# A two-layer gated Flamingo block on one Trainium2 core: the second attention's keys and values are made between the products of the first FFN, and its slot is written as one list per engine

## The chip, the cores and the metric

The kernel runs on one core of one Trainium2 chip, as one launch. The metric is device time in microseconds, the median over several executions. Matrix products in full precision are made here from two rounded parts of each operand (hi and lo) in three passes of TensorE.

## The reference, cut to what matters

```python
# x (16, 256, 256), ctx (16, 77, 256)
x = x + tanh(g_xattn[0]) * L0_xattn(layernorm(x), ctx)   # 16 heads of 16
x = x + tanh(g_ffn[0])   * L0_ffn(layernorm(x))          # quantised, hidden 768
x = x + tanh(g_xattn[1]) * L1_xattn(layernorm(x), ctx)   # 8 heads of 64
x = x + tanh(g_ffn[1])   * L1_ffn(layernorm(x))          # butterfly, hidden 1024

def L0_ffn(x):        # act_qdq: round(v / s) * s with s = max|v| / 32767 over the whole tensor
    x = act_qdq(x); up = act_qdq(x @ qdq(w_up).T); gate = act_qdq(x @ qdq(w_gate).T)
    gate = act_qdq(gate * u16(sigmoid(gate)))
    return act_qdq(gate * up) @ qdq(w_down).T
def L1_xattn(x, ctx): # no biases but bo
    q, k, v = x @ Wq, ctx @ Wk, ctx @ Wv                 # inner width 512
    return softmax(q k^T / 8) v @ Wo + bo
```

The keys and values of the second attention depend on ctx and the weights alone, so nothing of x has to be ready for them.

## The kernel before, in words

`build` calls four stages in order: the first attention (`stacked_attention`), the quantised FFN (`quantised_ffn`), the second attention (`attention` with layer=1) and the butterfly FFN (`butterfly_ffn`). x stays in SBUF as xres: 16 batches (b) of 256 rows, two tiles of 128. Each stage is a chain of blocks; in a block every engine has its own in-order program, and engines meet at semaphores. A block ends when all its engines have ended. A product of two fp32 operands is `three_passes` (L39 to L41): hi by hi, hi by lo, lo by hi.

**Down phase**, the last block of the quantised FFN (L2005 to L2178). f_hid holds the product of gate and up. Per batch DVE makes the codes (L2052, f_ocode), ACT rounds them to f_o_hi (L2093), DVE subtracts to f_o_lo (L2057), TensorE makes the down product of the batch, 2 tiles x 6 chunks x 3 passes = 36 matmuls, and DVE adds it to xres (L2064). Between these, ACT and POOL combine the outer butterfly matrices (f_y, f_z) for the last FFN (L2123, L2128, POOL's sums L2028); TensorE's nine small products for them stand around the first two batches. SP stores f_z and f_y to w_spill (L2034, L2036). hid is laid out by chunk: [128, 6, 4096].

**Setup** of the second attention (one block). SP loads the weights a_w_raw (L954), ctx a_c_raw (L958), a_wo_raw (L962) and small operands (bias, gate, mask, pick). ACT rounds, DVE splits (L1027 is ctx's lo part). TensorE makes 12 key products, 4 chunks of the inner width by 3 column groups of ctx (412, 410, 410 columns), each 6 matmuls; ACT and DVE keep them as a_k_hi (L1006) and a_k_lo (L1036). Then 16 value products, one per batch, 77 rows x 512, 6 matmuls each, copied by DVE to a_values (L1049), which POOL has cleared (L980). Meanwhile DVE and POOL make the layer norm of batch 0 (statistics L892, L897; inverse root L903, L905; normalised a_xn L910). ACT loads the table for Exp at L1009.

**Slot loop** (one block, `slots`). The 16 batches are run through a software pipeline. One slot is one list of steps, the same for every engine; an engine does those steps of it that are its own:

```python
            SLOT = ("s0 s1 xt kb p0 q0 at0 q1 s2 p1 mx0 at1 s3 mx1 p2 mx2 p3 mx3 ln pr0 norm mt xn pr1").split()
            slot(-1, 1, middle=False, back=False)
            slot(0, 0, back=False)
            with eng.Fori(0, (B - 4) // 2) as j:
                slot(j * 2 + 1, 1)
                slot(j * 2 + 2, 0)
            slot(B - 3, 1)
            slot(B - 2, 0, pre=False)
            slot(B - 1, 1, pre=False, front=False)
            slot(B, 0, pre=False, front=False, middle=False)
```

In slot b the scores and sums of batch b are made; ln and xn belong to batch b+2, the front steps (xt, kb, q, mx, mt) to batch b+1, the back steps (at, pr) to batch b-1. The steps are: ln, statistics of x on DVE (L892, L897) and their inverse root on POOL (L903, L905); xn, the normalised rows on DVE (L910), after which POOL adds the gated bias to xres (L918); xt, four transposes of xn (TensorE L1356, ACT hi L1219, DVE lo L1287); q0 and q1, the queries in two halves of 12 x 2 matmuls (a_w_hi; ACT L1226, DVE L1296, two operations each); kb, the masked keys of the batch (DVE's hi half, POOL's lo half, both L1160); mx0 to mx3, a cheap single-pass score product (L1380) whose maxima over the 77 keys DVE takes (L1304); mt, their transposes (L1388), copied by ACT (L1231) to a_mt; s0 to s3, the scores of two heads each, in which a fourth matmul takes the maxima off (a_pick by a_mt), and their Exp on ACT (L1238, a_prob); p0 to p3, the sums over keys by values (L1417); norm, the division on DVE (L1260 to L1273); at0 and at1, transposes of the result (L1431, ACT L1243, DVE L1310); pr0 and pr1, the projection, 24 matmuls a half (a_wo_hi), whose result DVE adds to xres (L1318) in pr1. s0 waits for a_mt.

## Time and profile before

| what | value |
|---|---|
| median of 3 executions | 1223.14 us (1222.58 to 1225.68) |
| profiled execution, its own time | 1222.77 us |
| its span | 1221.0 us, mean granted TensorE clock 0.926 |
| busy: PE, DVE, ACT, POOL | 85%, 67%, 48%, 21% |
| down phase | 582 to 663 us |
| setup of the second attention | 667 to 717 us |
| its slots | 717 to 998 us |

Times in the rows are microseconds from the start of the span. Where an engine was idle before an instruction, the row ends with that idle time and what released it. The granted clock is a share of TensorE's full speed, 1.00 being 2.4 GHz.

### The profile page before, as it was taken

What the parts mean: (1) busy time and instruction counts of PE and PEld (TensorE: products, weight loads), DVE (VectorE), ACT (ScalarE), POOL (GpSimd) and SP (SyncE); (2) the same over time, 40 slices, a digit from 0 to 9 for tenths busy, and PEclk for the clock granted to TensorE, in tenths of its full rate; (3) what the DMA queues carried; (4) which work ended last, traced back from release to release, by engine and by line L of the source; (5) the groups of instructions that cost most, each with busy time, mean ns of one, the idle gap of its engine ahead of it and who ended that gap; (6) DMA issues with size and microseconds to landing.
All of it is one profiled execution on the core that took longest, in us unless ns stands there. A gap on an engine that the chain in (4) does not pass through costs nothing. (4 is left out here: it accounts for less than half of the span.)

```text
span 1221.0 us, 20807 instructions
## 1 busy us (share of the span) xinstructions
PE 1033.3 (85%) x7125; PEld 903.3 (74%) x7125; DVE 820.3 (67%) x1700; ACT 580.8 (48%) x1028; POOL 261.4 (21%) x454
## 2 busy tenths in 40 slices
PE   6499999998389988366996779999999967999998
PEld 5367777776378866256996658999999956888888
DVE  5357787864458898798685745666666638676562
ACT  3256666665377699697463403333333314232220
POOL 4313333311176000000023112222221203211110
PEclk9689999998689999677998889999999988999999
DMA  6735555561233177697001200000000020000001
GB/s 191 210 93 130 129 129 129 130 191 36 78 140 138 44 250 250 238 308 254 35 0 70 90 1 1 1 0 0 0 0 0 1 77 2 18 18 18 20 32 35
DMA packets 50765, 106.50 MB, mean 87 GB/s; under 512 B 6688, under 2 KB 25120, under 8 KB 48400
## 3 DMA queue, kind: packets, MB, share of 16 engines
q1 hardware_dynamic: 50400, 104.61, 27.3%
q0 software_dynamic: 304, 1.10, 0.3%
q8 instruction: 35, 0.57, 0.2%
q14 instruction: 26, 0.21, 0.1%
HBM read 63.64 MB, written 39.52 MB: 84 GB/s over the span
## 5 line engine op out<-in xcount | busy, mean ns | idle before, releaser
L39 PE MATMUL bank<-f_xt_hi,f_w_hi 128*128 128x512 f32 x320 | 130.6, 408 | 16.2 <-DMA f_xt_lo<-x_spill 9.5
L41 PE MATMUL bank<-f_xt_hi,f_w_lo 128*128 128x512 f32 x320 | 127.7, 399 | 0.0
L40 PE MATMUL bank<-f_xt_lo,f_w_hi 128*128 128x512 f32 x320 | 127.7, 399 | 0.0
L2370 ACT ACTIVATE f_h<-bank,f_b 128x512 f32<-128x512 f32 x64 | 43.3, 691 | 130.8 <-PE bank L41 80.9
L659 DVE TENSOR_REDUCE a_maxima<-bank 128x4 f32<-128x308 f32 x128 | 60.5, 472 | 46.3 <-PE bank L732 46.0
L593 ACT ACTIVATE a_prob<-bank 77x512 f32<-77x512 f32 x128 | 72.7, 592 | 33.0 <-PE bank L757 32.7
L39 PEld LDWEIGHTS bank<-f_xt_hi,f_w_hi 128*128 128x128 f32 x320 | 61.9, 193 | 33.1 <-DMA f_xt_lo<-x_spill 12.1
L39 PE MATMUL bank<-f_w_hi,f_h_hi 128*128 128x256 f32 x256 | 72.8, 284 | 7.7 <-DVE xres L2325 7.7
L754 PE MATMUL bank<-a_stack,a_kb 96*77 96x256 f32 x256 | 72.4, 305 | 4.7 <-ACT a_mt L586 4.7
L41 PE MATMUL bank<-f_w_hi,f_h_lo 128*128 128x256 f32 x256 | 72.2, 282 | 0.0
L40 PE MATMUL bank<-f_w_lo,f_h_hi 128*128 128x256 f32 x256 | 72.1, 282 | 0.0
L39 PE MATMUL bank<-a_xt_hi,a_w_hi 128*128 128x256 f32 x192 | 60.3, 314 | 14.0 <-DVE a_xt_lo L1287 11.2
L732 PEld LDWEIGHTS bank<-a_kb,a_stack 96*128 96x128 f32 x256 | 40.5, 199 | 42.6 <-DVE a_maxima L659 28.4
L41 PEld LDWEIGHTS bank<-f_xt_hi,f_w_lo 128*128 128x128 f32 x320 | 61.6, 192 | 13.9
L2028 POOL TENSOR_TENSOR f_y<-f_y,f_y_pair 128x1028 f32<-128x1028 f32 x6 | 15.7, 2645 | 259.6 <-ACT f_y L2128 259.6
L40 PEld LDWEIGHTS bank<-f_xt_lo,f_w_hi 128*128 128x128 f32 x320 | 61.9, 193 | 12.3
L757 PE MATMUL bank<-a_mt,a_pick 128*77 128x256 f32 x256 | 68.8, 291 | 0.0
L732 PE MATMUL bank<-a_kb,a_stack 96*128 96x156 f32 x256 | 58.4, 311 | 11.7 <-DVE a_maxima L659 4.4
L1417 PE MATMUL bank<-a_values,a_prob 128*128 (+1 forms) x512 | 65.3, 271 | 0.0
L1693 DVE TENSOR_REDUCE f_gmax<-f_hid 128x2 f32<-128x1024 f32 x48 | 55.6, 1213 | 13.9 <-ACT f_hid L1807 13.7
L1417 PEld LDWEIGHTS bank<-a_values,a_prob 128*128 128x128 f32 x512 | 62.3, 192 | 0.0
L39 PE MATMUL bank<-a_wo_hi,a_at_hi 128*128 128x256 f32 x192 | 59.0, 307 | 2.8 <-DVE a_at_lo L663 1.4
(268 smaller groups left out, 3228.2 us busy)
## 6 DMA issues: line engine op xcount, KB each, us to landing
u_spill<-f_ubuf SPq DMA_DIRECT2D x48, 256.0 KB, 2.2
f_uback<-u_spill SPq DMA_DIRECT2D x24, 512.0 KB, 5.7
a_stack<-a_queries SPq DMA_DIRECT2D x16, 512.0 KB, 5.1
f_mats<-in_low_steps SPq DMA_DIRECT2D x12, 512.0 KB, 6.9
xres<-in_x SPq DMA_DIRECT2D x16, 256.0 KB, 4.4
a_queries<-a_q_hi SPq DMA_DIRECT2D x16, 256.0 KB, 2.8
a_queries<-a_q_lo SPq DMA_DIRECT2D x16, 256.0 KB, 3.0
a_stack<-a_queries SPq DMA_DIRECT2D x16, 256.0 KB, 5.8
```

The source lines that it names most:

```text
L39: nc.tensor.matmul(out, w_hi, m_hi, start=start, stop=False)
L40: nc.tensor.matmul(out, w_hi, m_lo, start=False, stop=False)
L41: return nc.tensor.matmul(out, w_lo, m_hi, start=False, stop=stop)
L593: act.activation(prob[0:S, n % 4, :, :].rearrange("p a b -> p (a b)"), (S0, S1)[n % 2][0:S, :], ACT.Exp, scale=SCALE).then_inc(probs, 1)
L659: dve.tensor_reduce(maxima[:, t, 4 * k:4 * k + 4], MX[:, 0:4 * SE].rearrange("p (h s) -> p h s", s=SE)[:, :, 0:S], AX.X, ALU.max).then_inc ...
L732: last = pe.matmul(MX[:, 2 * n * SE:2 * (n + 1) * SE], stack[0:ROWS, par, pair, t * P:(t + 1) * P], kb[0:ROWS, par, :, pair, :], start=Tru ...
L754: pe.matmul(out, kb[0:ROWS, par, a, pair, 0:S], stack[0:ROWS, par, pair, :], start=True, stop=False)
L757: last = pe.matmul(out, pick[:, 2 * pair + a, 0:S], mt[:, par, :], start=False, stop=True)
L1417: last = pe.matmul(out_of(t, h), prob[:, n % 2, hh, t * P:(t + 1) * P], v, start=True, stop=True)
L1693: dve.tensor_reduce(gmax[:, side, m - 1:m + 1], hid[:, f - 1:f + 1, g * GT:(g + 1) * GT], AX.X, op).then_inc(g_maxed, 1)
L2028: pool.tensor_tensor(y[:, tiles, :], y[:, tiles, :], y_pair[:, tiles, :], ALU.add).then_inc(y_add, 1)
L2370: act.activation(h[:, n % 2, :], hbank[n % 4][:, :], ACT.Gelu, bias=b1[:, n:n + 1]).then_inc(h_ready, 1)
```

## The change

It has four parts.

1. **Layout.** hid is laid out by batch, [128, 16, 6, 256], at the right end of SBUF, and so is the spill of u in DRAM. As the down phase codes batch after batch, hid's place comes free from its first batch on, and `late_tensors` puts the second attention's tensors over it: ctx hi and lo, a raw buffer, the weights' parts and the values. Each is used only after as many batches are coded as cover it (raw 5, wk 7, wv 8, values 13, wq 15, wo 16).
2. **Down phase.** The loop over batches is written out. SP loads ctx and the weights in it; ACT rounds and DVE splits them. TensorE makes 12 key products (groups of 6, 6 and 4 batches, 462, 462 and 308 columns), two behind each down product 6 to 11, and ten value products (128 rows of ctx, 80 in the last), 3, 4 and 3 behind down products 12, 13 and 14. ACT and DVE write the keys' parts into two stages, and SP saves them to key_spill (24 saves of 128 x 6 or 4 rows of 308 bytes). ACT moves the values to two stages, two steps of b later; SP saves them to value_spill (ten saves) and fetches them again in two halves, behind the sixth and behind the last save. The store of f_y stands between the fourth and the fifth save.
3. **No setup block.** `late_attention` begins with its slots, one slot earlier (slot -2 with ln, xn and the key fetch of batch 0 alone). Pick, gate and bias are loaded there; ACT takes them after xn of batch 0.
4. **The slot**, now a list per engine. TensorE's steps stand in their old order. The masked keys are fetched by SP, two DMAs of 64 x 8 rows of 308 bytes a batch, into a cleared tensor (kb). ln has four operations on POOL (also -mean and -mean x rstd); xn is on ACT, two operations, ahead of mt; q has one operation of 512 columns on ACT and one on DVE; on DVE pr1 stands ahead of norm. The sums take 77 rows of prob and values, not 128.

The diff, cut to its core:

```diff
+def late_tensors(nc, late):
...
+    for name, shape, _ in shapes:
+        used += math.prod(shape[1:])
+        late[f"{name.split('_')[0]}_free"] = -(-used // per_batch)
...
-            SLOT = ("s0 s1 xt kb p0 q0 at0 q1 s2 p1 mx0 at1 s3 mx1 p2 mx2 p3 mx3 ln pr0 norm mt xn pr1").split()
...
+        PE_SLOT = "s0 s1 xt p0 q0 at0 q1 s2 p1 mx0 at1 s3 mx1 p2 mx2 p3 mx3 pr0 mt pr1".split()
+        ACT_SLOT = "s0 s1 xt q0 at0 q1 s2 at1 s3 xn mt".split()
+        DVE_SLOT = "xt q0 at0 q1 mx0 at1 mx1 mx2 mx3 ln pr1 norm".split()
+        POOL_SLOT = "ln xn".split()
+        SP_SLOT = "kb".split()
...
+            slot(-2, 0, front=False, middle=False, back=False)
             slot(-1, 1, middle=False, back=False)
...
+                    pool.wait_ge(ln_stats, b + 1)
+                    pool.tensor_tensor(nmean[:], zero[:], mv[:, :, 0], ALU.subtract)
+                    pool.tensor_tensor(var[:], mv[:, :, 1], eps[:], ALU.add).then_inc(ln_eps, 1)
+                    pool.wait_ge(ln_eps, b + 1)
+                    if not (isinstance(b, int) and b == 0):
+
+                        pool.wait_ge(ln_xn, b)
+                    pool.tensor_tensor(rstd[:], var[:], minus_half[:], ALU.pow).then_inc(ln_rstd, 1)
+                    pool.wait_ge(ln_rstd, b + 1)
+                    pool.tensor_tensor(nmr[:], nmean[:], rstd[:], ALU.mult).then_inc(ln_nmr, 1)
...
+                if what == "xn":
+                    act.wait_ge(ln_nmr, b + 1)
+                    if not (isinstance(b, int) and b == 0):
+
+                        act.wait_ge(xt_ready, b)
+                    for t in range(TT):
+                        last = act.activation(xn[:, t, :], xtile(b, t), ACT.Identity, bias=nmr[:, t:t + 1],
+                                              scale=rstd[:, t:t + 1])
+                    last.then_inc(ln_xn, 1)
+                    if isinstance(b, int) and b == 0:
+                        act.wait_ge(small_in, 48)
+                        act.activation(tg[:], gate_raw[:], ACT.Tanh).then_inc(g_done, 1)
+                        act.activation(pick[:], pick_raw[:], ACT.Copy).then_inc(picked, 1)
+                        act.activation(warm[:], gate_raw[:], ACT.Exp)
...
-        hid = sb("hid", [P, FT, NT * P])
+        late = env["late"]
+        hid_stack = ExitStack()
+        hid = hid_stack.enter_context(nc.sbuf_tensor("f0_hid", [P, B, FT, T], F32, side="right"))
...
-                    sp.dma_start(env["u_dram"][:, f, g * GT:(g + 1) * GT], ubuf[:, u % NU, :]).then_inc(u_sent[u % NU], 16)
+                    sp.dma_start(env["u_dram"][:, 2 * g:2 * g + 2, f, :],
+                                 ubuf[:, u % NU, :].rearrange("p (b t) -> p b t", t=T)).then_inc(u_sent[u % NU], 16)
...
+            GROUPS = [(0, 6), (6, 6), (12, 4)]
+            KEYS = [(c, b0, nb) for b0, nb in GROUPS for c in range(C)]
+            NK = len(KEYS)
+            NV = -(-B * S // P)
...
+            KEYS_AT = [6 + n // 2 for n in range(NK)]
+            VALUES_AT = [12, 12, 12, 13, 13, 13, 13, 14, 14, 14]
...
+                def save_key(n):
+                    c, b0, nb = KEYS[n]
+                    for part, made in enumerate((k_rounded, k_done)):
+                        sp.wait_ge(made, n + 1)
+                        sp.dma_start(late["k_dram"][:, b0:b0 + nb, part, c, :],
+                                     k_stage[:, n % 2, part, 0:nb * S].bitcast(F32).rearrange("p (b s) -> p b s", s=S),
+                                     ).then_inc(k_saved[n % 2], 16)
+
+                def save_values(i):
+                    sp.wait_ge(v_done, i + 1)
+                    at = v_rows(i)
+                    sp.dma_start(late["v_dram"][at, :],
+                                 v_stage[0:at.stop - at.start, i % 2, :, :].rearrange("p h v -> p (h v)"),
+                                 ).then_inc(v_saved[i % 2], 16)
+
+                def fetch_values(half, stored):
+                    for n in range(2):
+                        sp.wait_ge(v_saved[n], 16 * ((stored + 1 - n) // 2))
+                    sp.wait_ge(ocoded, late["values_free"])
+                    bs = slice(half * B // 2, (half + 1) * B // 2)
+                    sp.dma_start(late["values"][0:S, bs, :, :].rearrange("p b h v -> p b (h v)"),
+                                 late["v_dram"][bs.start * S:bs.stop * S, :].rearrange("(b s) n -> s b n", s=S),
+                                 ).then_inc(late["values_in"], 16)
+
+                sp.wait_ge(ocoded, late["raw_free"])
+                for n, (b0, nb) in enumerate(GROUPS):
+                    src = late["ctx_t"][:, b0 * S:(b0 + nb) * S]
+                    sp.dma_start(c_raw(n), src.rearrange("(c p) n -> p c n", p=P)).then_inc(c_in[n], 16)
+                sp.wait_ge(l_split["c"], 2)
+                weight("wk")
+                sp.wait_ge(l_split["c"], 3)
+                weight("wv")
                 sp.wait_ge(unit_out, len(UNITS))
                 sp.dma_start(bf["w2_dram"], z[:]).then_inc(z_stored, 16)
-                sp.wait_ge(y_add, 2 * TOP)
-                sp.dma_start(bf["w1_dram"], y[:]).then_inc(y_stored, 16)
+                for n in range(NK):
+                    save_key(n)
+                sp.wait_ge(l_split["wk"], 1)
+                weight("wq")
+                sp.wait_ge(l_split["wv"], 1)
+                weight("wo")
+                for n in range(2):
+                    sp.wait_ge(k_saved[n], 16 * NK)
+                for i in range(NV):
+                    save_values(i)
+                    if i == 3:
+                        sp.wait_ge(y_add, 2 * TOP)
+                        sp.dma_start(bf["w1_dram"], y[:]).then_inc(y_stored, 16)
+                    if i == NV // 2:
+                        fetch_values(0, i)
+                fetch_values(1, NV)
...
+                    if b in (2, 3):
+                        split_context(b - 2)
+                    if b == 3:
+                        split_context(2)
+                    if b == 4:
+                        split_late("wk")
+                    if b == 5:
+                        split_late("wv")
+                    if b == 12:
+                        split_late("wq")
+                    if b == 13:
+                        split_late("wo")
+                    for n in range(NK):
+                        if KEYS_AT[n] == b:
+                            split_key(n)
...
+                for b in range(4, B + 2):
+                    if b < B:
+                        hi(b)
+                    for n in range(NK):
+                        if KEYS_AT[n] == b - 2:
+                            round_key(n)
+                    for i in range(NV):
+                        if VALUES_AT[i] == b - 2:
+                            move_values(i)
+                    if b in (4, 5):
+                        round_context(b - 4)
+                    if b == 5:
+                        round_context(2)
+                    if b == 6:
+                        round_late("wk")
+                    if b == 7:
+                        round_late("wv")
+                    if b == 14:
+                        round_late("wq")
+                    if b == 15:
+                        round_late("wo")
...
+                    prod(b)
+                    for n in range(NK):
+                        if KEYS_AT[n] == b:
+                            key_product(n)
+                    for i in range(NV):
+                        if VALUES_AT[i] == b:
+                            value_product(i)
...
-               "u_dram": nc.dram_tensor("u_spill", (P, HID0 // P, NT * P), F32, kind="Internal").ap()}
+               "u_dram": nc.dram_tensor("u_spill", (P, B, HID0 // P, T), F32, kind="Internal").ap()}
...
                           a["gx0"], a["picks0"], a["ctx_t"], a["x"])
-        quantised_ffn(nc, env, env["ffn_weights"]["quantised"], a["gf0"], butterfly)
-        attention(nc, env, 1, 8, 512, a["wqkv1"], a["wo1"], None, None, None, a["bo1"], a["gx1"],
-                  a["ctx_t"], None)
+        with ExitStack() as late_stack:
+            env["late"] = {"ctx_t": a["ctx_t"], "wqkv": a["wqkv1"], "wo": a["wo1"], "stack": late_stack}
+            quantised_ffn(nc, env, env["ffn_weights"]["quantised"], a["gf0"], butterfly)
```

The order of instructions shows the moves. On ACT, in the slot loop (a_prob is the Exp of scores, a_mt the step mt, a_xt_hi xt, a_q_hi q, a_at_hi at). Before:

```order
L1226 ACTIVATE a_q_hi<-bank 128x256 x2
L1238 ACTIVATE a_prob<-bank 77x512
L1243 ACTIVATE a_at_hi<-bank 128x512
L1238 ACTIVATE a_prob<-bank 77x512
L1231 ACTIVATE a_mt<-bank 8x256
L1238 ACTIVATE a_prob<-bank 77x512 x2
```

and now, in the slot after the loop:

```order
L1042 ACTIVATE a_q_hi<-bank 128x512
L1055 ACTIVATE a_prob<-bank 77x512
L1060 ACTIVATE a_at_hi<-bank 128x512
L1055 ACTIVATE a_prob<-bank 77x512
L1028 ACTIVATE a_xn<-xres,a_nmr,a_rstd 128x256 x2
L1048 ACTIVATE a_mt<-bank 8x256
L1055 ACTIVATE a_prob<-bank 77x512 x2
```

Two a_xn, which DVE had before, stand between the last Exp of the slot and a_mt.

On DVE, at the end of a slot (a_maxima is mx, a_bn and a_mv are ln, a_rden and a_att norm, xres the addition of pr1). Before:

```order
L1304 TENSOR_REDUCE a_maxima<-bank 128x4
...
L892 BN_STATS a_bn<-xres 128x6
...
L897 BN_AGGR a_mv<-a_bn 128x2 x2
L1260 RECIPROCAL a_rden<-bank 128x7
...
L1269 TENSOR_TENSOR a_att<-bank,a_rden 128x448
L1273 TENSOR_SCALAR a_att<-bank,a_rden 128x64
L910 TENSOR_SCALAR a_xn<-xres,a_mv,a_rstd 128x256 x2
...
L1318 SCALAR_TENSOR_TENSOR xres<-bank,a_tg,xres 128x256
```

and now, in the last slots:

```order
L1121 TENSOR_REDUCE a_maxima<-bank 128x4 x3
L1135 SCALAR_TENSOR_TENSOR xres<-bank,a_tg,xres 128x256 x2
L1076 RECIPROCAL a_rden<-bank 128x7
L1077 RECIPROCAL a_rden<-bank 128x1
L1076 RECIPROCAL a_rden<-bank 128x7
L1077 RECIPROCAL a_rden<-bank 128x1
L1083 TENSOR_TENSOR a_att<-bank,a_rden 128x448
L1085 TENSOR_SCALAR a_att<-bank,a_rden 128x64
L1083 TENSOR_TENSOR a_att<-bank,a_rden 128x448
L1085 TENSOR_SCALAR a_att<-bank,a_rden 128x64
```

The addition to xres moved from behind the division to ahead of it.

On SP, in the down phase (a_raw is ctx, then the weights; f_z and f_blocks are where the stages of keys and values lie). Before, down phase and setup:

```order
L2034 DMA w_spill<-f_z 128x2048
L2036 DMA w_spill<-f_y 128x2056
...
L954 DMA a_w_raw<-in_wqkv 128x2x512
L958 DMA a_c_raw<-in_ctx_t 128x2x412
L958 DMA a_c_raw<-in_ctx_t 128x2x410 x2
L954 DMA a_w_raw<-in_wqkv 128x2x512 x2
L962 DMA a_wo_raw<-in_wo 128x4x256
```

and now, in the down phase alone:

```order
L1906 DMA a_raw<-in_ctx_t 128x2x462 x2
L1906 DMA a_raw<-in_ctx_t 128x2x308
L1877 DMA a_raw<-in_wqkv 128x2x512 x2
L1912 DMA w_spill<-f_z 128x2048
L1883 DMA a_key_spill<-f_z 128x6x77 x16
L1883 DMA a_key_spill<-f_z 128x4x77 x8
L1877 DMA a_raw<-in_wqkv 128x2x512
L1877 DMA a_raw<-in_wo 128x4x256
L1890 DMA a_value_spill<-f_blocks 128x520 x4
L1925 DMA w_spill<-f_y 128x2056
L1890 DMA a_value_spill<-f_blocks 128x520 x2
L1899 DMA a_values<-a_value_spill 77x8x520
```

Behind these stand three saves, the save of the last 80 rows and the second fetch into a_values; all are in one queue with the store of f_y.

## Rows read from the trace of the kernel before

**Rows 1.** Stretches: length; PE, PEld, DVE, ACT, POOL busy; clock, DMA share, GB/s.

```profile
585.00:625.00 40.00, 38.14 (x296) 37.52 (x295) 29.41 (x30) 21.89 (x32) 5.49 (x2) 0.97 0.07 27
765.00:960.00 195.00, 187.61 (x1609) 185.42 (x1609) 127.29 (x373) 67.71 (x144) 47.98 (x96) 1.00 0.00 0
```

**Rows 2.** Timeline, first down matmul and last addition: start, busy, engine, line, operation.

```profile
582.14 0.39 PE L39 MATMUL bank<-f_d_hi,f_o_hi 128*128 128x256 f32 x1 [2.17 <-DVE f_o_lo L2057]
...
662.21 0.88 DVE L2064 SCALAR_TENSOR_TENSOR xres<-bank,f_back,xres 128x256 f32<-128x256 f32 x2 [3.44 <-PE bank L41]
```

**Rows 3.** Timeline of a pause in the down phase, and stretches behind two pauses.

```profile
623.75 0.42 PE L39 MATMUL bank<-f_d_hi,f_o_hi 128*128 128x256 f32 x1 [1.86 <-DVE f_o_lo L2057]
...
625.00:628.00 3.00, 3.00 (x19) 3.00 (x18) 2.84 (x4) 1.78 (x5) 0.00 (x0) 0.61 0.00 0
...
646.00:650.00 4.00, 4.00 (x35) 4.00 (x35) 3.84 (x6) 2.37 (x6) 0.00 (x0) 1.00 0.00 0
```

**Rows 4.** Setup: key splits, value copies (ns, first to last start), a memset, the table load.

```profile
L1036 DVE SCALAR_TENSOR_TENSOR a_k_lo<-bank,a_k_hi x6: 584/584/586, 689.0 to 694.7; 128x410 fp32r<-128x410 f32 x6
...
L1049 DVE COPY a_values<-bank x13: 686/687/687, 699.7 to 716.3; 77x512 f32<-77x512 f32 x13
...
669.17 7.02 POOL L980 MEMSET a_values<- 128x8320 f32 x1
...
694.64 1.28 ACT L1009 ACT_TABLE_LOAD   x1
```

**Rows 5.** Timeline, slot -1: q0, mx3, s0.

```profile
720.12 0.58 PE L39 MATMUL bank<-a_xt_hi,a_w_hi 128*128 128x256 f32 x1 [2.01 <-DVE a_xt_lo L1287]
...
730.26 0.71 PE L1380 MATMUL bank<-a_kb_hi,a_q_hi 128*128 128x154 f32 x2 [0.57 <-DVE a_maxima L1304]
...
732.60 0.50 PE L39 MATMUL bank<-a_q_hi,a_kb_hi 128*77 128x256 f32 x1 [0.46 <-ACT a_mt L1231]
```

**Rows 6.** Timeline of a steady slot, from mx3 to the next s0, and xt_lo's wait.

```profile
843.29 0.43 PE L1380 MATMUL bank<-a_kb_hi,a_q_hi 128*128 128x154 f32 x2
...
845.05 0.25 DVE L897 BATCH_NORM_AGGREGATE a_mv<-a_bn 128x2 f32<-128x6 f32 x2 [0.15 <-DVE a_bn L892]
...
845.44 0.37 ACT L1231 ACTIVATE a_mt<-bank 8x256 fp32r<-8x256 f32 x1 [3.52 <-PE bank L1388]
...
846.67 0.28 PE L39 MATMUL bank<-a_q_hi,a_kb_hi 128*77 128x256 f32 x1
...
847.04 0.72 DVE L910 TENSOR_SCALAR a_xn<-xres,a_mv,a_rstd 128x256 f32 x2
...
850.62 0.39 PE L39 MATMUL bank<-a_xt_hi,a_w_hi 128*128 128x256 f32 x1 [0.62 <-DVE a_xt_lo L1287]
```

**Rows 7.** Timeline, first attention: the same norm with POOL's four operations, xn on ACT.

```profile
153.03 1.08 ACT L196 ACTIVATE a_xn<-xres,a_nmr,a_rstd 128x256 f32 x2
153.39 0.25 DVE L686 BATCH_NORM_AGGREGATE a_mv<-a_bn 128x2 f32<-128x6 f32 x2 [0.18 <-DVE a_bn L678]
...
154.92 0.20 POOL L560 TENSOR_TENSOR a_nmr<-a_nmean,a_rstd 128x2 f32<-128x2 f32 x1
```

**Rows 8.** DMA issues: queue, KB each, median us to landing.

```profile
u_spill<-f_ubuf SPq DMA_DIRECT2D x48, 256.0 KB, 2.2
...
a_keys<-a_k_hi SPq DMA_DIRECT2D x1, 1248.0 KB, 6.9
a_keys<-a_k_lo SPq DMA_DIRECT2D x1, 1248.0 KB, 10.3
...
w_spill<-f_y SPq DMA_DIRECT2D x1, 1028.0 KB, 3.9
...
a_pick_raw<-in_pick SPq DMA_DIRECT2D x1, 312.0 KB, 8.4
```

**Rows 9.** Timeline: end of the division, addition of pr1, and at0 of batch 15.

```profile
846.85 0.27 DVE L1273 TENSOR_SCALAR a_att<-bank,a_rden 128x64 f32<-128x64 f32 x1
...
847.68 0.87 DVE L1318 SCALAR_TENSOR_TENSOR xres<-bank,a_tg,xres 128x256 f32 x2
...
988.93 0.63 PE L1431 MATMUL bank<-ident,a_att 128*128 128x128 f32 x4 [1.06 <-DVE xres L1318]
```

More of the change, by code:

```diff
@@ new lines, in _, with step @@
+            sp.dma_start(gate_raw[:], gate).then_inc(small_in, 16)
+            sp.dma_start(bo_raw[:], gbias).then_inc(small_in, 16)
+            def step(what, b, par):
+                if isinstance(b, int) and b < 2:
+                    if b == 0:
+                        sp.wait_ge(kb_cleared, 1)
+                else:
+                    sp.wait_ge(scores, (b - 1) * HP)
+                    sp.sem_inc(sp_passed, 1)
+                for a in range(HPC):
+                    rows = slice(a * d, (a + 1) * d)
+                    sp.dma_start(kb[rows, par, :, :, a, :].bitcast(F32).rearrange("p n c s -> p (n c) s"),
+                                 late["k_dram"][rows, bass.ds(b, 1), :, :, :].rearrange("p o n c s -> p (o n c) s"),
+                                 ).then_inc(keys_in[par], 16)
@@ L1218, in step @@
                     act.wait_ge(xt_ready, b + 1)
                     act.activation(xt_hi[:], T0[:, :], ACT.Copy).then_inc(xt_rounded, 1)
[L1220 removed]
+                elif what in ("q0", "q1"):
                     n = int(what[1])
                     act.wait_ge(q_ready, b * NP + n + 1)
[L1223 to L1228 removed]
+                    act.activation(q_hi[:, par, 2 * n:2 * n + 2, :].rearrange("p a b -> p (a b)"), (T0, X0)[n][:, :],
+                                   ACT.Copy).then_inc(q_rounded, 1)
@@ new lines, in step @@
+                    for t in range(TT):
+                        last = dve.bn_stats(bn[:, t, :], xtile(b, t))
+                    last.then_inc(ln_bn, 1)
+                    dve.wait_ge(ln_bn, b + 1)
+                    if not (isinstance(b, int) and b == 0):
+                        dve.wait_ge(ln_nmr, b)
+                    dve.sem_inc(passed, 1)
+                    for t in range(TT):
+                        last = dve.bn_aggr(mv[:, t, :], bn[:, t, :])
+                    last.then_inc(ln_stats, 1)
@@ L1387, in step @@
                     for t in range(TT):
-                        last = pe.transpose(T0[0:heads, t * P:(t + 1) * P], maxima[:, t, :], ident[:])
+                        last = pe.transpose(T0[0:HEADS, t * P:(t + 1) * P], maxima[:, t, :], ident[:])
                     last.then_inc(mt_ready, 1)
-                elif what[0] == "s" and what[1] != "t":
+                elif what in ("s0", "s1", "s2", "s3"):
                     n = int(what[1])
@@ L1410, in step @@
                     if n == 0:
-                        pe.wait_ge(att_ready, b)
-                    for hh in range(2):
-                        h = 2 * n + hh
+                        if isinstance(b, int) and b == 0:
+                            pe.wait_ge(values_in, 32)
+                        else:
+                            pe.wait_ge(att_ready, b)
+                    for a in range(2):
+                        h = 2 * n + a
                         for t in range(TT):
-                            v = values[:, bass.ds(b, 1), h, :].rearrange("p o v -> p (o v)")
-                            last = pe.matmul(out_of(t, h), prob[:, n % 2, hh, t * P:(t + 1) * P], v,
+                            v = values[0:S, bass.ds(b, 1), h, :].rearrange("p o v -> p (o v)")
+                            last = pe.matmul(out_of(t, h), prob[0:S, n % 2, a, t * P:(t + 1) * P], v,
                                              start=True, stop=True)
                     last.then_inc(outs, 1)
-                elif what[:2] == "at":
+                elif what in ("at0", "at1"):
                     n = int(what[2])
@@ L1433, in step @@
                     last.then_inc(at_ready, 1)
-                elif what[:2] == "pr":
+                elif what in ("pr0", "pr1"):
                     t = int(what[2])
@@ L1443, in step @@
                         last.then_inc(proj_ready, 1)
-            slots(pe, step)
+            slots(pe, PE_SLOT, step)
     free_semaphores(nc, sems)
```

707 lines of the change are left out of this document (280 added, 427 removed).

## The prediction, on record before the changed kernel was run

> **What bounds the kernel now.** I read the table of stretches first. In the down phase TensorE is busy 38.14 of 40 us, and in the loop of the second attention 187.61 of 195 us at granted clock 1.00 [rows 1]: work added to TensorE in either lengthens the program, work removed shortens it. The first down matmul starts at 582.14 and the last addition ends at 662.21 + 0.88 = 663.1 [rows 2]; the reader should take both as the borders of what the change touches first. The next first score matmul (s0) starts at 732.60 [rows 5]. Between them lie 69.5 us of setup, in which the slot loop cannot begin: raw loads, rounding, 12 key products, 16 value products, then the first slot. The slots that follow are the third place. Everything before 582 is taken as unchanged: the spill of u has 1 KB runs instead of long ones and lands beside ACT-bound work, and the butterfly FFN is only shifted.
>
> **1. Products moved into the down phase.** A key product of 410 columns is paced 5.7 us / 5 = 1.13 us, a value product of 77 x 512 at 16.6 / 12 = 1.38 [rows 4]. The change makes eight of 462 columns (1.27 each), four of 308 (0.85) and ten value products of 128 rows, whose columns are still 512 (1.39): 10.2 + 3.4 + 13.9 = **+27.3 us** on an engine that is 95% busy. The pauses of the phase cost 3.7 us in the trace, one of them the 1.86 us at 623.75 [rows 3]; the change spreads the work that POOL's additions delay, but adds waits for wk. I take them as equal; bounds -5 (all pauses filled) and +3 (twice the wait).
>
> **2. The end of that block.** SP must have saved all values and issued the second fetch. It is one queue in order. From the end of product 13: ACT moves the fifth value product after the rounding of codes and of wo, +7.1; the store of y, 3.9 [rows 8], with saves 4 and 5 behind it landing at +13.8; fetch of the first half of values, as many bytes as one save of a_k_hi, 6.9 and 0.5 of issue, +21.2; saves 6 and 7 queued behind it 1.6, moves of the last 0.7, last save 2.8 and issue 0.5: +26.8. TensorE needs from there 4 x 1.39 + 4.31 + 3 x 1.39 + 4.31 = 18.4 and the addition 0.9. So SP is **+7.5 us** later than the engines. Bounds: 0, if the fetch does not delay the small saves (they land in 2.2 as u_spill does [rows 8]), and +11.5, if y and the fetch share the engines at the rate of a_k_lo, 10.3.
>
> **3. The setup goes.** Block start to start 3.85 us stays. Then DVE's statistics and four small POOL operations; POOL has first to clear kb and mt, 2,976 columns at 7.02 us per 8,320 [rows 4], 2.5 and two starts: 2.95. Normalising takes 1.5 and 1.08 [rows 7], the transposes 0.6. ACT meanwhile takes the gate and pick and loads the table for Exp, 1.28 [rows 4], to about 8.5 us; rounding and splitting xt 0.6 + 0.7: q0 at 10.0. From q0 to s0 the trace has 732.60 - 720.12 = 12.48 [rows 5], and part 4 adds 2.95. 3.85 + 10.0 + 12.48 + 2.95 = 29.3 against 69.5: **-40.1 us**. Bounds 27 (gate and pick land early) and 34 (they land 8.4 us after issue, as pick did among six loads).
>
> **4. The slot.** The list of operations for TensorE keeps its order. On ACT, xn (normalised x, formerly DVE at 847.04) now stands ahead of mt, the rounding of the maxima that s0 waits for. In the steady slot the trace has mx3 843.29, the aggregate of the statistics 845.05, mt on ACT 845.44, s0 846.67 [rows 6]: 3.38 us from mx3 to s0, filled with projection matmuls, and mt has 0.86 us of room. The new chain is: aggregate ends 845.30; POOL's var, rstd, nmr take from 153.39 + 0.25 to 154.92 + 0.20, 1.48 us with releases [rows 7], to 846.78; two xn on ACT 1.04 to 1.08 [rows 7], 847.86; mt 0.37 and 0.1 to release: s0 at 848.33, that is **+1.66 us in each of 13 slots, +21.6**. Behind the waiting mt stands ACT's s0's exp only, so nothing else is late. In slot -1, where mx3 stands at 730.26 and s0 2.34 later [rows 5], the same chain takes 5.2: +2.95 (in part 3), and slot 0 has the same order: **+3.05**. Removed from the slot: DVE's masked keys and xn, POOL's lo half of the masked keys, four q operations for two; none ends a wait of TensorE but the 0.62 at q0 behind xt_lo, which keeps its chain. The two key fetches per slot, 2 x 512 rows of 308 bytes, land within microseconds in a 16 us slot.
>
> **5. DVE's order at the end.** The addition pr1 (847.68, [rows 9]) now stands ahead of the division norm (1.9 us, ending 847.12). In a full slot the division still ends 0.4 before p0 needs it. In slots 14 and 15 p0 and at0 follow at once: at 988.93 TensorE waited 1.06 for the addition; with the division behind it +1.95, and +1.5 in the slot before: **+3.5**.
>
> **Sum.** 27.3 + 7.5 - 40.1 + 3.05 + 21.6 + 3.5 = **+22.9 us**. The profiled execution took 1222.77 (span 1221.0), 0.4 below the median of 1223.14, so the forecast is 1222.8 + 22.9, about 1246.
>
> **Rivals.**
> *A, faster.* The slots lose nothing: POOL's chain or xn is done before mt's own input, because the aggregate or ACT comes earlier than I read. mt must end by 846.6 to cost nothing, so POOL's chain and the two xn must take at most 0.93 us from the aggregate's end at 845.30 (846.6 - 845.30 - 0.37), where the rows give 1.48 + 1.04 = 2.52; or the aggregate must come 1.6 us earlier. For it: DVE is relieved of masked keys and xn, and could be ahead. Against: the statistics stand behind the last maxima of the slot, which wait for mx3. Then 27.3 + 7.5 - 40.1 + 0.7 = -4.6: 1218; 1211 with part 2 at nothing as well. Below +0.3 us per slot the kernel is no slower. Chance 0.10.
> *B, the 308-byte rows.* 16,384 key rows go out beside the down products, 1,024 per DMA engine. Rows of 624 bytes took 10.3 us for 256 per engine, 40 ns a row [rows 8]. If the price is per byte it is 20 ns: 21 us; if per row 41 us; against six batch steps of 6.8 us = 41. Forecast: hidden. If a row costs 60 ns, key products wait for free stages: 61 - 41 = +20, 1266. The nearest rows speak for at most 40. Chance 0.08. The Trainium skill's page "DMA: Bandwidth & Descriptors", in the table at its top, says that transfers under 512 bytes are done as read-modify-write; no row here shows such a write. By the page's rule, with each row at twice the 40 ns, the saves take 82 us against 41, an estimate of +41: 1287; as a mechanism of this kernel that is TensorE waiting at each key product from the third on for a stage not yet saved. Chance 0.04.
> *C, the clock.* After the 1.86 us pause at 623.75 the granted clock of 625 to 628 was 0.61, with 19 matmuls in 3 us; after a like pause at 644 it stayed 1.00 [rows 3]. The slots have it at 1.00 [rows 1]. If the pause of 1.66 us in each slot lowers it for some microseconds, 1 to 2 us more are lost per slot, +13 to +22: 1258 to 1268. Chance 0.15.
> *D, the change does not do what it says.* The fetch of values or the free stages hold the loop so that the setup is not removed: the block's end at +11.5 and first s0 at 34: 9 us over the forecast, 1255. Chance 0.08. That leaves 0.55 for the forecast.
>
> **How the numbers follow.** Likeliest: 1246. Its own bounds: part 1 -5 or +3, part 2 -7.5 or +4, part 3 -2 or +5, part 4 from +1.2 to +1.9 a slot, -6 or +3: together, taken as independent, some -11 and +8. The range 1229 to 1267 takes in D, C and most of B. A measurement of this kernel can tell 0.3%, 3.7 us, from none. Faster by more than that: most of A, 0.08. Within: the rest of A and the forecast with all bounds low, 0.05. Slower: 0.87.
>
> **What would show it.** In the trace after: s0 in a steady slot starts behind ACT's mt, with mt behind xn, about 5.0 us after mx3; the period is 17.9 instead of 16.3 us. The down phase ends near 116 us after its first matmul instead of 81, with TensorE idle at its end behind SP. The time from block end to first s0 is below 34. The forecast is wrong if mt starts at its old place relative to mx3 (A), if TensorE waits at key products for rounding that waits on a save (B), or if the clock in the slots falls below 0.9 (C).

## The result: 2.9% slower, and the profile after

| | before | changed |
|---|---|---|
| median, 4 executions each | 1222.86 us | 1258.69 us (1253.23 to 1263.71) |
| ratio, 95% interval | | 1.0286 (1.0256 to 1.0315) |
| profiled execution: own time, span | 1222.77, 1221.0 | 1253.23, 1251.3 |
| mean granted clock | 0.926 | 0.921 |
| TensorE busy | 1033.3 us, 85% | 1032.2 us, 82% |

The change is +35.8 us by the medians and +30.3 us by the two profiled spans. The profiled execution of the changed kernel is the fastest of its four, so the account below, made from spans, is on the low side; the rest is taken up at the end.

The stages are cut at the same events in both traces: the first down matmul, the end of the last addition of the down phase, the first statistics of the next block, mt of slot -1 (its first matmul on TensorE), mt of slot 14, the end of the last addition to xres. Stretches in us:

| stretch | before | changed | difference | forecast |
|---|---|---|---|---|
| start to first down matmul | 582.14 | 580.00 | -2.1 | 0 |
| down phase, to the last addition | 80.95 | 117.39 | +36.4 | +27.3 |
| from there to the next block's first statistics | 3.83 | 5.39 | +1.6 | +7.5 |
| to mt of slot -1 | 64.62 | 22.61 | -42.0 | -43.1 |
| mt of slot -1 to mt of slot 14, 15 slots | 243.50 | 275.38 | +31.9 | +29 |
| to the end of the last addition | 23.35 | 27.97 | +4.6 | +2 |
| butterfly FFN | 222.61 | 222.60 | 0.0 | 0 |

(The forecast's -40.1 for the setup holds the 2.95 of slot -1, which stands in the slots here, and of the 3.5 at the end 1.5 lies before mt of slot 14.) The slots and the setup came close to their terms; the down phase came out 9.1 us above its term, the end of the block 5.9 below, and the end of the loop 2.6 above.

**The steady slot.** Timeline of the changed kernel from mx3 to the next s0, which answers to [rows 6] (columns: start, us, engine, line, operation, count, idle before and its releaser):

```profile
835.88 0.43 PE L1176 MATMUL bank<-a_kb,a_q_hi 128*128 128x154 f32 x2
...
837.61 0.38 PE L1183 MATMUL bank<-ident,a_maxima 128*8 128x128 f32 x2
837.66 0.25 DVE L1100 BATCH_NORM_AGGREGATE a_mv<-a_bn 128x2 f32<-128x6 f32 x2 [0.17 <-DVE a_bn L1092]
...
839.26 0.19 POOL L1008 TENSOR_TENSOR a_nmr<-a_nmean,a_rstd 128x2 f32<-128x2 f32 x1
...
839.59 1.09 ACT L1028 ACTIVATE a_xn<-xres,a_nmr,a_rstd 128x256 f32 x2 [5.09 <-POOL a_nmr L1008]
...
840.59 0.36 ACT L1048 ACTIVATE a_mt<-bank 8x256 fp32r<-8x256 f32 x1
...
841.08 0.34 PE L40 MATMUL bank<-a_q_hi,a_kb 128*77 128x256 f32 x1 [1.66 <-ACT a_mt L1048]
```

TensorE has the maxima turned at 837.99, but mt follows at 840.59: ACT stood 5.09 us for POOL's nmr, made xn, and only then took mt. From mx3 to s0 it is 5.20 us where [rows 6] had 3.38, and the period is 18.17 instead of 16.27. TensorE's waits from 760 to 960 (total, times, longest):

```profile
PE bank L40 <- ACT a_mt L1048: 18.7, 11, 1.9
PE bank L40 <- DVE a_xt_lo L1107: 6.8, 11, 0.6
```

The second line is the old wait at q0. The granted clock stayed at 1.00 in spite of a pause in every slot (changed kernel; length, PE, PEld, DVE, ACT, POOL busy, clock, DMA share, GB/s):

```profile
850.00:900.00 50.00, 43.14 (x365) 42.00 (x365) 24.52 (x66) 17.38 (x33) 7.99 (x18) 1.00 0.09 19
```

**The down phase.** The same columns for the whole phase, changed kernel, and below it what ACT waited for in it:

```profile
585.00:697.00 112.00, 102.49 (x697) 96.11 (x696) 70.90 (x77) 57.55 (x93) 19.09 (x7) 0.95 0.59 125
```

```profile
ACT f_z L2040 <- DMA a_key_spill<-f_z: 25.5, 8, 4.3
ACT f_blocks L2051 <- DMA a_value_spill<-f_blocks: 17.6, 4, 6.8
```

The reader should see two things. TensorE is idle for 9.5 of 112 us (before 3.7 of 76), and ACT stands 25.5 us in eight waits before it can round the next keys (L2040), because the stage it writes to has not been saved yet. ACT is in order: behind those waits stand the rounding of codes that the down products need. TensorE's own waits in the phase say so:

```profile
PE bank L40 <- DVE f_o_lo L1949: 6.2, 4, 2.4
PE bank L40 <- ACT f_blocks L2051: 2.3, 1, 2.3
```

The DMA view of the same kernel from 615 to 675 (queue: packets, MB, share of 16 engines; then issues: KB, us to landing):

```profile
q1 hardware_dynamic: 16942, 5.88, 69.7%
...
a_key_spill<-f_z SPq DMA_DIRECT2D x16, 231.0 KB, 6.0
a_key_spill<-f_z SPq DMA_DIRECT2D x8, 154.0 KB, 4.8
```

16,942 packets on 16 engines are 1,059 each, in 69.7% of 60 us = 41.8 us: 39.5 ns a packet, nearly all of 308 bytes. This mean looks like the 40 ns of a 624-byte row [rows 8], but it mixes two prices. The same line in the first microsecond of the first key save (623 to 624), and in a stretch behind three saves that SP issued between 626.9 and 628 (629.5 to 632). In both every packet is under 512 bytes:

```profile
q1 hardware_dynamic: 732, 0.22, 93.1%
...
q1 hardware_dynamic: 948, 0.29, 140.4%
```

Worked out as above, a row takes 20 ns in the first and 59 ns in the second (the share passes 100% because packets of one engine overlap there), and the rows moved fell from 732 a microsecond to 379. So a short row of the first save costs half of a 624-byte row, as its bytes do. The three saves begin at this price too (1,226 rows from 627.5 to 629.5), and then a row costs three times as much. The Trainium skill ("DMA: Bandwidth & Descriptors", Specifications) puts a loss under 512 bytes down to a read-modify-write. The trace shows a loss in the queued saves and none in the first; what causes it no run here shows.

### The profile page after: what moved, and what is told of

Read it like the earlier page. It is cut to its first block and busy times, and to the rows that moved or that the text cites. A ratio compares the mean times of both kernels' runs of the same rounds, so it can differ in the third digit from the quotient of the medians.

```text
span 1251.3 us, 20623 instructions
## 1 busy us (share of the span) xinstructions
PE 1032.2 (82%) x7089; PEld 903.3 (72%) x7089; DVE 773.0 (62%) x1556; ACT 597.2 (48%) x1038; POOL 236.7 (19%) x422
## 5 line engine op out<-in xcount | busy, mean ns | idle before, releaser
L41 PEld LDWEIGHTS bank<-f_xt_lo,f_w_hi 128*128 128x128 f32 x320 | 62.2, 194 | 12.4
L1215 PE MATMUL bank<-a_values,a_prob 77*128 (+1 forms) x512 | 66.0, 273 | 1.0 <-DVE a_att L1085 1.0
L40 PE MATMUL bank<-f_d_hi,f_o_hi 128*128 128x256 f32 x192 | 57.3, 298 | 8.4 <-DVE f_o_lo L1949 8.4
L1215 PEld LDWEIGHTS bank<-a_values,a_prob 77*128 77x128 f32 x512 | 63.0, 194 | 1.3 <-ACT a_prob L1055 1.3
L1493 DVE TENSOR_REDUCE f_gmax<-f_hid 128x1 f32<-128x1024 f32 x48 | 55.6, 1212 | 12.6 <-ACT f_hid L1607 12.4
L40 PE MATMUL bank<-a_q_hi,a_kb 128*77 128x256 f32 x128 | 39.2, 306 | 28.7 <-ACT a_mt L1048 28.7
```

The lines of the kernel that those rows point to most:

```text
L40: nc.tensor.matmul(out, w_hi, m_hi, start=start, stop=False)
L41: nc.tensor.matmul(out, w_hi, m_lo, start=False, stop=False)
L1215: last = pe.matmul(out_of(t, h), prob[0:S, n % 2, a, t * P:(t + 1) * P], v, start=True, stop=True)
L1493: dve.tensor_reduce(gmax[:, side, m // 2:m // 2 + 1], hid[:, 2 * g:2 * g + 2, f - 1:f + 1, :], AX.XYZ, op).then_inc(g_maxed, 1)
```

## The experiments

Nine kernels ran. Medians, with the ratio to the kernel before on the same chip:

| kernel | median us | ratio (95%) |
|---|---|---|
| changed | 1258.69 | 1.0286 (1.0256 to 1.0315) |
| 1 mt first | 1232.33 | 1.0056 (1.0028 to 1.0083) |
| 2 norm first | 1260.30 | 1.0287 (1.0216 to 1.0358) |
| 3 key rows | 1250.08 | 1.0215 (1.0157 to 1.0272) |
| 4 y early | 1262.33 | 1.0314 (1.0261 to 1.0367) |
| 5 = 1 + 3 | 1217.85 | 0.9956 (0.9928 to 0.9984) |
| 6 = 1 + 2 + 3 | 1212.14 | 0.9898 (0.9863 to 0.9934) |
| 7 = 6 + gate late | 1205.87 | 0.9844 (0.9811 to 0.9878) |
| 8 = 7 + clear late | 1207.47 | 0.9846 (0.9806 to 0.9885) |
| 9 = 7 + y early | 1208.98 | 0.9858 (0.9821 to 0.9896) |

Their stretches, from the profiled execution of each, cut as above (us):

| kernel | down | to next block | to mt(-1) | 15 slots | steady period | tail |
|---|---|---|---|---|---|---|
| before | 80.95 | 3.83 | 64.62 | 243.50 | 16.27 | 23.35 |
| changed | 117.39 | 5.39 | 22.61 | 275.38 | 18.17 | 27.97 |
| 1 | 120.30 | 5.91 | 23.68 | 248.41 | 16.53 | 27.52 |
| 2 | 120.23 | 5.68 | 21.92 | 280.39 | 18.17 | 24.44 |
| 3 | 107.82 | 5.61 | 24.26 | 276.71 | 18.17 | 28.12 |
| 4 | 122.37 | 4.59 | 24.08 | 278.91 | 18.17 | 27.00 |
| 5 | 107.18 | 5.53 | 24.20 | 246.41 | 16.53 | 28.24 |
| 6 | 108.05 | 5.67 | 23.76 | 245.52 | 16.28 | 23.59 |
| 7 | 107.15 | 5.34 | 18.67 | 244.60 | 16.28 | 24.45 |
| 8 | 108.02 | 5.41 | 17.86 | 243.55 | 16.28 | 24.44 |
| 9 | 107.52 | 7.36 | 19.06 | 243.49 | 16.28 | 24.45 |

### 1. mt ahead of xn on ACT

```diff
-        ACT_SLOT = "s0 s1 xt q0 at0 q1 s2 at1 s3 xn mt".split()
+        ACT_SLOT = "s0 s1 xt q0 at0 q1 s2 at1 s3 mt xn".split()
```

> The changed kernel with one move: on ACT, mt stands ahead of xn in the slot. Theory (mt queued behind xn, which waits for POOL's four operations, is what lengthens the slot): the wait of 1.66 us before s0 goes, the period falls from 18.17 to 16.3 to 16.5 us, slots -1 and 0 win 3 each; in all -28 to -31 us, to about 1229. Rival (the slot is long because xn itself is late, whoever makes it, and the transposes xt behind it only hide that): with mt first xn ends at the same place, the wait moves from s0 to xt, the period stays above 17.5 and the time above 1247.

The slots fell by 27.0 us, the median by 26.4. Timeline of this kernel at the same place, and TensorE's only wait from 760 to 970:

```profile
848.73 0.38 PE L1183 MATMUL bank<-ident,a_maxima 128*8 128x128 f32 x2
...
849.15 0.37 ACT L1048 ACTIVATE a_mt<-bank 8x256 fp32r<-8x256 f32 x1 [3.51 <-PE bank L1183]
...
850.38 0.28 PE L40 MATMUL bank<-a_q_hi,a_kb 128*77 128x256 f32 x1
...
850.73 1.09 ACT L1028 ACTIVATE a_xn<-xres,a_nmr,a_rstd 128x256 f32 x2 [1.21 <-POOL a_nmr L1008]
```

```profile
PE bank L1215 <- DVE a_att L1085: 10.3, 13, 0.8
```

mt now comes at once when TensorE has turned the maxima, and s0 follows without a pause. xn is as late as before relative to the statistics, and TensorE's transposes do not notice it: the rival, that a late xn lengthens the slot whoever waits for it, falls. What is left over the kernel before, 0.26 us a period, is a new wait at p0 for the division (a_att), 0.8 us each: the division stands behind pr1's addition, which was covered as long as the slot was long.

### 2. norm ahead of pr1 on DVE

```diff
-        DVE_SLOT = "xt q0 at0 q1 mx0 at1 mx1 mx2 mx3 ln pr1 norm".split()
+        DVE_SLOT = "xt q0 at0 q1 mx0 at1 mx1 mx2 mx3 ln norm pr1".split()
```

> The changed kernel with one move: on DVE, norm stands ahead of pr1, as before the change. Theory (the division behind the addition is seen only where no scores follow, in slots 14 and 15 and at the start): -3.5 to -5 us, to about 1254.5, at an unchanged period of 18.17. Rival (the division ahead delays the addition and with it at0 and the bias of the next norm): no gain, 1258 to 1262.

By the median nothing came of it (1260.30). By the stretches the tail (from mt of slot 14 on) is 3.5 us shorter, as the theory has it, at an unchanged period; the slots as a whole are 5.0 us longer, and all of that lies in the first four of them (see the clock, below). Experiment 4, whose slots are the changed kernel's own, is 3.5 us longer in the same place, so most of the 5.0 need not be the edit's. The gain in the tail is there and too small to be seen beside that spread. In experiments 5 and 6 the same pair is told apart more clearly.

### 3. Key saves in one run per partition

```diff
-    late["k_dram"] = nc.dram_tensor("a1_key_spill", (P, B, 2, C, S), F32, kind="Internal").ap()
+    late["k_dram"] = nc.dram_tensor("a1_key_spill", (P, 2, C, B, S), F32, kind="Internal").ap()
...
-                        sp.dma_start(late["k_dram"][:, b0:b0 + nb, part, c, :],
+                        sp.dma_start(late["k_dram"][:, part, c, b0:b0 + nb, :],
```

(and the fetch of a batch's keys, which reads the same runs of 308 bytes, follows the layout).

> The changed kernel with the key spill laid out so that a save writes one run of 1848 (or 1232) bytes per partition, not 6 (or 4) of 308; the fetches still read 308-byte runs. Theory (ACT stands waiting for key saves, 25.5 us in 8 waits, and so rounds codes late for the down product): those waits fall under 5 us, TensorE's idle time in the phase from 9 to 4, fewer spells of low clock; -5 to -8 us, to about 1252. Rival (the pauses come from POOL's sums, which slow DVE, as before the change): ACT's waits fall but TensorE's pauses stay, 0 to -1 us.

The down phase fell from 117.39 us (and 120.3, 120.2, 122.4 in experiments 1, 2 and 4, which leave it as it is) to 107.82. The DMA issues from 615 to 670, ACT's wait and TensorE's wait in the phase:

```profile
a_key_spill<-f_z SPq DMA_DIRECT2D x16, 231.0 KB, 2.4
a_key_spill<-f_z SPq DMA_DIRECT2D x8, 154.0 KB, 2.0
```

```profile
  DMA a_key_spill<-f_z: 9.0, 8
```

```profile
PE bank L40 <- DVE f_o_lo L1949: 2.6, 2, 2.4
```

The same bytes land in 2.4 us instead of 6.0, and from the first key save to the last it is 38.7 us instead of 49.2. ACT's wait fell from 25.5 to 9.0, less than expected, but enough that it no longer reaches TensorE, whose one long pause of 2.4 us stands before the first key save, beside POOL's sums, as in [rows 3]. The rival, that POOL's sums make all the pauses, falls for the rest of them. 107.82 is +26.9 over the kernel before, and the first term of the forecast, the products alone, was +27.3. The waits of TensorE make up 6.4 of the 9.6 us won; the rest goes with fewer pauses and spells at a lower clock (0.95 over the phase in the changed kernel, 0.98 here). By the medians the edit gives 8.6 us, with intervals that overlap a little; on top of mt first (experiment 5 against 1) it takes the ratio from 1.0056 to 0.9956, and there the intervals are apart. The whole phase here:

```profile
585.00:688.00 103.00, 99.23 (x703) 94.34 (x701) 71.22 (x77) 58.23 (x94) 19.15 (x7) 0.98 0.39 136
```

### 4. f_y stored ahead of the first save of values

```diff
                 for i in range(NV):
-                    save_values(i)
-                    if i == 3:
+                    if i == 0:
                         sp.wait_ge(y_add, 2 * TOP)
                         sp.dma_start(bf["w1_dram"], y[:]).then_inc(y_stored, 16)
+                    save_values(i)
```

> The changed kernel with the store of f_y ahead of the first save of values, not between the fourth and the fifth. Theory (the end of the block is SP's chain of saves and fetches, in which the store's 1 MB stands): the block's end comes 2 to 4 us earlier relative to TensorE's last down product, 1255 to 1257. Rival (the last saves wait for ACT's moves at the end of the products anyway): under 1 us.

No gain: the next block starts 4.59 us behind the last addition, not 5.39, but the phase before it was 122.37 long. The first saves of values now stand behind the store, and TensorE's wait for ACT's move of the values, 2.3 us in the changed kernel, is 5.4:

```profile
PE bank L40 <- ACT f_blocks L2051: 5.4, 1, 5.4
```

What the block's end won was lost ahead of it. Experiment 9 tries the same edit where TensorE has no such wait.

### 5 and 6. The cures together, without and with norm first

> The changed kernel with mt ahead of xn on ACT and the key saves in one run per partition; DVE's pr1 still ahead of norm. If the two costs are independent their gains add: slots near 248, down phase near 108, span about 1218 to 1222, within 0.5% of the kernel before. If not (the shorter down phase hands over to a slower clock in the first slots, or SP's end of block takes over), the sum comes out 4 us or more above that.

> The same with norm ahead of pr1 on DVE as well. With mt first, TensorE waited 0.8 us a slot at p0 for the division. Theory: that wait goes, the period falls from 16.53 to 16.2 or less, the tail from 27.5 to 24.4: 6 to 8 us under the run with pr1 first, span about 1212, 0.5 to 1% faster than the kernel before. Rival (xn on ACT holds the exponentials, which then are what p0 waits for): the wait only changes its name, period 16.5, gain 3 us from the tail alone.

Both gains added up: 1217.85 us, span 1216.0, a ratio of 0.9956 whose interval leaves out 1, by little. With norm first as well, 1212.14: the period fell from 16.53 to 16.28, the wait for a_att is gone and the old one at q0 is back as the only one (TensorE's waits, 755 to 960, experiment 6):

```profile
PE bank L40 <- DVE a_xt_lo L1107: 7.9, 13, 0.6
```

The tail went from 28.24 to 23.59. So DVE's order cost 4.7 us at the end of the loop, and another 0.25 a slot as soon as the slot was short. Slot 0 (18.12 against 16.56) took part of it back in this one trace.

### 7. Gate, pick and table behind the rounding of xt

```diff
                     last.then_inc(ln_xn, 1)
-                    if isinstance(b, int) and b == 0:
-                        act.wait_ge(small_in, 48)
-                        act.activation(tg[:], gate_raw[:], ACT.Tanh).then_inc(g_done, 1)
-                        act.activation(pick[:], pick_raw[:], ACT.Copy).then_inc(picked, 1)
-                        act.activation(warm[:], gate_raw[:], ACT.Exp)
                 elif what == "xt":
                     act.wait_ge(xt_ready, b + 1)
                     act.activation(xt_hi[:], T0[:, :], ACT.Copy).then_inc(xt_rounded, 1)
+                    if isinstance(b, int) and b == 0:
+                        act.wait_ge(small_in, 48)
+                        act.activation(tg[:], gate_raw[:], ACT.Tanh).then_inc(g_done, 1)
+                        act.activation(pick[:], pick_raw[:], ACT.Copy).then_inc(picked, 1)
+                        act.activation(warm[:], gate_raw[:], ACT.Exp)
```

(and the gated bias on DVE behind its split of xt.)

> The same with tanh of the gate, pick and the Exp table taken on ACT behind the rounding of xt of batch 0, not ahead of it (and the gated bias on DVE behind the split). Theory (the first query product waits 5.2 us because ACT first waits for pick, gate and bias to land and loads the table): first products 3 us earlier, -2.5 to -3.5 us. Rival (the table and pick are then late for the first scores): under 1 us.

In the changed kernel ACT held the rounding of xt back: it stood 2.81 us for the small loads, then loaded the table, while the transposes had ended at 709.15.

```profile
710.79 0.20 ACT L1033 ACTIVATE a_tg<-a_gate_raw 128x1 f32<-128x1 f32 x1 [2.81 <-DMA a_bo_raw<-in_bo]
710.90 0.71 ACT L1034 ACTIVATE a_pick<-a_pick_raw 128x624 fp32r<-128x624 f32 x1
711.62 1.28 ACT L1035 ACT_TABLE_LOAD   x1
712.91 0.20 ACT L1035 ACTIVATE a_warm<-a_gate_raw 128x1 f32<-128x1 f32 x1
713.02 0.58 ACT L1038 ACTIVATE a_xt_hi<-bank 128x512 fp32r<-128x512 f32 x1
```

TensorE's wait for the split of xt (total, times, longest), 690 to 755, in experiment 6 and in this one:

```profile
PE bank L40 <- DVE a_xt_lo L1107: 7.1, 3, 6.0
...
PE bank L40 <- DVE a_xt_lo L1104: 3.0, 4, 1.4
```

Behind the rounding all of it is covered by TensorE's 24 query matmuls: 18.67 us to mt(-1) instead of 23.76, and 6.3 us by the median, where 2.5 to 3.5 were expected. 4.6 of the 5.1 us are the longest wait, 6.0 before and 1.4 now; the last 1.2 us of the median lie outside this stretch and are not explained. This version, 1205.87 us, beats both kernels: 1.6% under the one before.

### 8 and 9. Two edits without effect

```diff
-            pool.memset(kb[:].bitcast(F32), 0.0).then_inc(kb_cleared, 1)
...
                     pool.tensor_tensor(nmr[:], nmean[:], rstd[:], ALU.mult).then_inc(ln_nmr, 1)
+                    if isinstance(b, int) and b == 0:
+                        pool.memset(kb[:].bitcast(F32), 0.0).then_inc(kb_cleared, 1)
+                        pool.memset(mt[:].bitcast(F32), 0.0).then_inc(mt_cleared, 1)
```

> The version with mt first, norm first, key rows and late gate; POOL clears kb and mt behind the four operations of batch 0's norm, not ahead of them. Theory (the first xn of the new block waits for POOL's 2.8 us of clearing): first xn 2.5 to 3 us earlier, block start to mt(-1) from 18.7 to about 16, -2 to -3 us. Rival (the transposes are then held by something else, or the keys, which wait for the clearing, arrive late for mx0): under 1 us.

> The version with mt first, norm first, key rows and late gate; the store of f_y ahead of the first save of values. In the changed kernel this edit gained nothing, with 308-byte rows in the queues. Theory (with the short queues the block's end is SP's chain of value saves and fetches, 3.4 us behind the last addition): block end 1 to 3 us earlier. Rival (ACT's last moves wait for saves 6 and 7, which stand behind the first fetch and not behind the store): within 1 us of the version without it.

With the clearing behind the norm, the first statistics to mt(-1) took 17.86 us, 0.8 less, and the time is the same as in 7. ACT's first xn came 2.74 us behind the statistics instead of 4.12: 1.4 us earlier and not the 2.5 to 3 expected, because POOL then waits 1.26 us for DVE's statistics. 0.6 of the 1.4 us was lost again on the way to mt(-1); what remains is too small for this measurement. The store of f_y ahead of the values (the edit of experiment 4, on 7) put the block's end at 7.36, not earlier: the store's megabyte then delays the first saves (ACT waits 8.3 us for one of them), and ACT's last two moves still wait 6.8 us for saves 6 and 7, queued behind the first fetch, as its rival had it.

## Why the prediction was right, and where its terms were off

The direction stood, and so did the mechanism of the slots. The size is in part luck: forecast +23 (1246, range 1229 to 1267), measured +35.8, 1258.69. That is above the 1254 which the forecast's own bounds allowed (+8), and within the range because the range made room for rivals B, C and D. Part of what came was the cost of B, and the block's end, 5.9 us under its term, hid some of it. The down phase of "near 116 us" met 117.39 by luck too: 116 was to hold 7.5 us in which TensorE stands behind SP.

- **Slots** (part 4, +1.66 each): right as to cause and place, shown by experiment 1, which gives 27.0 of 31.9 us back. The chain was 1.54 us on POOL, 1.09 for xn and 0.36 for mt, against 1.48, 1.04 to 1.08 and 0.37 in the working. The period rose by 1.90: s0 came 1.82 later, and 0.1 is spread over the slot. 13 x 0.24 = 3.1 us were missing in the term.
- **Products** (part 1, +27.3; its three addends make 27.5): right as to TensorE's work, +26.9 and +26.2 in experiments 3 and 5. What failed is the sentence beside it, that the pauses before and after are equal (TensorE's waits went from 3.7 to 9.0 us), and with it rival B's reading that the saves stay hidden. The row price of 40 ns was right as a mean alone (39.5): it is 20 ns in the first save and 59 in a queue of saves, near the 60 that B made its condition. And 41 us of rows against six batch steps of 41 us was no cover: the saves were issued over 49.2 us. Two stages hand over in order: a save starts only when ACT and DVE have written it, takes 6 us to land, and the ACT that waits for it also rounds the codes of the down products. A mean rate that just fits leaves every wait on the path of the next step. This is rival B, given 0.08, at about half of its +20: +9.6 us against the changed kernel's own trace, 12.4 to 14.6 against those of experiments 1, 2 and 4. Its path was another than the one written down: TensorE stood not at the key products for free stages (0.5 us), but at the down products for codes that ACT had not yet rounded (6.2). B's dearer case, +41 at 80 ns a row (given 0.04), did not come.
- **End of the block** (part 2, +7.5): mis-sized. It is +1.6. Two errors: the block before did not end with its last addition either, since SP waited there for the store of f_y that was issued at 661.59 and took 3.9 [rows 8], to 665.5; and the changed block's TensorE was itself late. In experiment 7 TensorE is not late, and there SP's chain from the end of down product 13 (671.53) to the second fetch (issued by 694.14) took 22.6 us where the working has 26.8: the fifth value product was moved 3.9 us behind down product 13, not 7.1. SP is behind by 3.4 us (last addition 690.71).
- **Setup** (part 3): -42.0 where the terms gave -43.1. q0 waited for gate, pick and table as worked out (11.6 us behind the first statistics, where the working has 10.0 from the block's start), and experiment 7 shows 5 us of it to be avoidable.
- **End of the loop** (part 5, +3.5, 2 of it in the tail): +4.6 in the tail; experiments 5 and 6 put 4.7 on DVE's order.
- **Rival A** fell: the chain from the aggregate's end took 2.8 us (837.91 to 840.68) where 0.93 was allowed. Had mt stood first, as in experiment 5 with the key rows mended, the time would be 1217.85. That this is near the 1218 worked out for rival A is chance: A had +7.5 for the block's end, which is +1.7 in experiment 5, and nothing for the end of the loop, which is +4.9. **Rival C**, the clock in the steady slots, fell: 1.00. (Its 1 to 2 us in 13 slots make +13 to +26, not +22.)

Left over between the profiled +30.3 and the medians' +35.8: 5.5 us. Executions of the same instructions differ by about as much. Experiment 4 has the changed kernel's slots, and its first two took 20.54 and 22.22 us against 18.98 and 20.32 in the changed kernel's own trace, 3.5 us more. Experiment 1 has the changed kernel's down phase, and it took 120.30 us against 117.39, with 582.35 against 580.00 ahead of it, 5.3 us more. What makes executions differ stays open.

## What the runs showed that was not expected

The clock in the first slots. In the kernel before it is 1.00 from 682 up to the end of the value products, 0.69 from 717 to 733 and 0.94 from 733 to 765. After the change TensorE has stood 11.5 us for the first xn when it starts, and the clock is low in most of the next 45 us: at 1.2 GHz from 701 to 718, from 721 to 735 and from 745 to 752, and at 2.4 GHz between and behind them. The clock of a longer stretch is a mean of the two. Stretches of the changed kernel, of experiment 2 and of experiment 7 (length, busy time of the five engines, then the clock):

```profile
720.00:740.00 20.00, 13.80 (x78) 12.41 (x79) 5.31 (x12) 4.92 (x9) 2.66 (x6) 0.66 0.00 1
740.00:765.00 25.00, 20.19 (x159) 19.57 (x159) 10.71 (x29) 7.08 (x13) 2.65 (x6) 0.86 0.12 26
```

```profile
720.00:740.00 20.00, 9.59 (x47) 8.30 (x48) 5.16 (x12) 5.61 (x10) 4.06 (x8) 0.67 0.06 9
740.00:765.00 25.00, 20.77 (x125) 20.33 (x124) 7.39 (x20) 6.71 (x12) 2.66 (x6) 0.70 0.06 14
```

```profile
715.00:740.00 25.00, 22.48 (x157) 21.38 (x156) 8.62 (x25) 9.63 (x18) 5.33 (x12) 0.82 0.06 14
740.00:765.00 25.00, 24.38 (x213) 24.17 (x212) 13.94 (x40) 9.25 (x17) 3.00 (x8) 1.00 0.13 26
```

Low clock and pauses go together: where mt first leaves short pauses in the first slots, the second slot takes 16.6 to 18.1 us, where xn first leaves pauses of 3.4 and 3.7, it takes 20.3 to 22.2. (A pause of 1.7 to 1.9 us in each steady slot went with 1.00.) Which of the two makes the other was not tried apart, and why it differs between executions stays open.

## What to carry to other kernels

On an in-order engine, look at what a moved step waits for, not at how long it is: xn costs ACT 1.1 us and had room, but its wait for POOL stood ahead of a 0.4 us copy that TensorE needed, and exchanging two words of a list was worth 26 us. A transfer whose rate just fits beside other work is not hidden when its stages are handed back through an engine that others wait for; here the layout of the spill, one run per partition, cut the landing from 6.0 to 2.4 us and gave 10 us back. And a step found to be covered is covered for that length of slot only: the division behind the addition cost nothing at 18.2 us a slot and 0.25 us a slot at 16.3.
